# Densely packed edge tiles with per-product tables in a graph transformer layer (gather of 128 message rows per tile, one Trainium2 core)

## What is computed

```python
xn = _layernorm(x, axis=-1)
# graph part: for each edge, HW[col] weighted, added into row
HW = xn @ gnn_W
msgs = edge_weight[:, None] * HW[dst]
AHW = jax.ops.segment_sum(msgs, src, num_segments=N_NODES)
# mix part: q and k through elu+1, k_sum, context = k^T v per head, out = (q context) / (q k_sum), Wproj
x = x + (AHW + gnn_b) + mix(xn, Wq, Wkv, Wproj, bproj)
x = x + ffn(_layernorm(x))      # top 2 of 8 experts, relu
```

## Time and profile before

| | |
|---|---|
| time, median of 3 runs | 3924.36 us (3923.73 to 3926.85) |
| the profiled execution, its own time | 3922.77 us |
| its span (first to last instruction) | 3920.7 us |
| PE busy | 2907.9 us (74%) |
| DVE busy | 2601.0 us (66%) |
| POOL busy | 2537.6 us (65%) |
| ACT busy | 639.4 us (16%) |
| mean granted clock of TensorE | 0.90 of full speed |

### The profile page before, as it was taken

The page is one execution under the profiler, slowest core; times in us unless marked ns, Lnnn a source line. Parts: engine busy times, 40 slices in busy tenths (PEclk is TensorE's granted clock), DMA queues, the critical chain, the costliest instruction groups (busy, mean ns, idle before and its releaser), DMA issues.

```text
span 3920.7 us, 56671 instructions
## 1 busy us (share of the span) xinstructions
PE 2907.9 (74%) x16402; PEld 2390.4 (61%) x16407; DVE 2601.0 (66%) x6332; ACT 639.4 (16%) x1334; POOL 2537.6 (65%) x2431
## 2 busy tenths in 40 slices
PE   5957767376766676766777777777665599999998
PEld 5846666255555555555555555555442488888887
DVE  8899888165555555557888888888767344444444
ACT  8222222310000000000000000000023122222221
POOL 0038888467777777777777777777735777544444
PEclk9997877789898989898998989989877799999999
DMA  5857775634444444434444444444364455544443
GB/s 171 277 166 223 209 212 163 191 105 116 119 119 119 119 118 118 119 114 131 130 130 130 127 128 131 129 131 127 110 209 143 118 119 120 96 72 71 73 71 56
DMA packets 363113, 522.66 MB, mean 133 GB/s; under 512 B 69241, under 2 KB 282749, under 8 KB 363005
## 3 DMA queue, kind: packets, MB, share of 16 engines
q0 software_dynamic: 130944, 275.64, 28.0%
q1 hardware_dynamic: 181523, 190.28, 16.4%
q10 hardware_dynamic: 50537, 55.32, 4.5%
HBM read 378.21 MB, written 140.28 MB: 132 GB/s over the span
## 4 chain that ended last, share of the span: by engine, by line
PE 49%; DVE 12%; issue 10%; POOL 4%; DMA 4%; DVEq 1%; ACT 0%; SPq 0%; POOLq 0%
PE bank L1261 15%; PE bank L1463 10%; PE bank L1476 10%; DVE relu_kq L1951 4%; PE bank L1267 4%; DVE acc L1864 4%; PE bank L1364 4%; DMA message<-h_table,gather_stage 3%; PE bank L1342 2%; POOL x_sorted L781 2%; POOL message L738 2%; PE bank L1362 2%; DVE select L1857 1%; PE bank L1450 1%; DMA read_back<-lists 1%
## 5 line engine op out<-in xcount | busy, mean ns | idle before, releaser
L738 POOL DMA_INDIRECT message<-h_table,gather_stage x1660 | 1598.5, 963 | 558.3 <-issue 488.0
L1261 PE MATMUL bank<-message,select 128*128 128x256 f32 x3320 | 896.8, 418 | 359.4 <-issue 287.8
L1864 DVE TENSOR_TENSOR acc<-acc,bank 128x256 f32 x1660 | 698.9, 421 | 554.3 <-PE bank L1261 390.1
L1261 PEld LDWEIGHTS bank<-message,select 128*128 128x128 f32 x3320 | 661.1, 207 | 553.2 <-issue 368.3
L699 POOL DMA_INDIRECT lists<-placed,dest_i x300 | 381.3, 1271 | 330.1 <-ACT placed L920 244.4
L792 POOL DMA_INDIRECT out<-acc,row_of x224 | 350.1, 1563 | 344.9 <-DVE acc L2157 270.5
L1857 DVE TENSOR_SCALAR select<-iota_n,gather_stage 128x128 f32<-128x128 f32 x1660 | 467.8, 360 | 3.3
L1463 PE MATMUL bank<-fx_t,acc 128*128 128x256 f32 x1792 | 407.6, 381 | 1.6 <-ACT fx_t L1054 1.6
L1476 PE MATMUL bank<-w,acc 128*128 x1792 | 405.2, 379 | 0.0
L1463 PEld LDWEIGHTS bank<-fx_t,acc 128*128 128x128 f32 x1792 | 342.1, 191 | 49.0 <-issue 2.1
L1476 PEld LDWEIGHTS bank<-w,acc 128*128 128x128 f32 x1792 | 331.9, 190 | 40.6
(11 more groups left out here) (304 smaller groups left out, 3648.7 us busy)
## 6 DMA issues: line engine op xcount, KB each, us to landing
rows<-block_dram SPq DMA_DIRECT2D x75, 514.5 KB
acc<-x_sorted SPq DMA_DIRECT2D x112, 260.0 KB, 2.8
message<-h_table,gather_stage POOLq DMA_INDIRECT x1660
xt_in<-xt_dram SPq DMA_DIRECT2D x98, 256.0 KB, 2.9
x_sorted<-blank_rows ACTq DMA_DIRECT2D x42, 390.0 KB
lists<-zeros_list SPq DMA_DIRECT2D x8, 1664.0 KB, 15.4
read_back<-lists SPq DMA_DIRECT2D x13, 1024.0 KB, 6.7
x_sorted<-blank_rows SPq DMA_DIRECT2D x2, 6370.0 KB
```

The costliest lines, as they stand in the source:

```text
L738: pool.indirect_dma_start(out=message[:, slot % SETS, j, :], out_offset=None, in_=h_table, in_offset=Offset(ap=gather_stage[:, slot, j, 0: ...
L1261: last = nc.tensor.matmul(ps, select[:, slot % 2, j, :], message[:, slot % SETS, j, :], start=True, stop=True)
L1864: added = V.tensor_tensor(to, to, ps, ALU.add)
```

## The change

**Packing.** A block now begins at a multiple of 16 edges (`UNIT`) in the sorted list instead of 128. The tiles lie densely: `DENSE` = 1575 tiles hold all edges, and one more, which is empty, serves as filler, so 1576 tiles are gathered, in 394 sets (`GSETS`). A tile may hold edges of two or more blocks. It is then multiplied once per block, each time with another selection matrix. The number of products is fixed at `TT` = 1672, in 418 sets. The row number of an edge in its record now has 10 bits (block modulo 8, and row), and the selection compares it with a 128-column window of a 1024-column ramp (`iota_n`), which starts at the block's key.

**Tables.** Which tile, which block and which message slot a product uses is no longer known when the kernel is written. DVE makes six rows of integers on the chip (`rows_of`), one word per product or set: `acc_row` (offset in `acc`), `key_row` (window of the ramp), `record_row` (where the tile's records lie), `message_row` (its slot in `message`), `need_row` (how far each of the four message semaphores must be), and `free_row` (from which product set on a gathered set's slot is free). They are made behind part 0 of the records (`product_rows`), ahead of the other parts.

**Use.** DVE loads four keys and four record places into registers at the head of each set, ahead of its selects, beside the load of offsets that was there. PE loads four message places and four counts ahead of each set's products. POOL loads eight counts every eight sets; its 394 sets are written out one by one instead of in a loop, and it reads `records` directly. SP's copies into `gather_stage` are gone.

```diff
-    TT = -(-((NG * P + NB * (P - 1)) // P) // SET) * SET
+    UNIT, KEYS = 16, 8
+    DENSE = -(-((E + NB * UNIT) // UNIT) // (P // UNIT))
+    GATHERS = -(-(DENSE + 1) // SET) * SET
+    GSETS = GATHERS // SET
+    TT = -(-(DENSE + NB - 1) // SET) * SET
...
+def load_counts(eng, registers, held, row, first, count, low, op_max):
+    eng.load(registers, row[0:1, first:first + count] if isinstance(first, int) else row[0:1, DynSlice(first, count)])
+    for r, h in zip(registers, held):
+        eng.reg_alu(h, r, low, op_max)
+    return held
...
-            with pool.Fori(1, TSETS // RING) as i:
-                for slot in range(RING):
-                    pool.wait_ge(s_list[slot // SETS], i * 16 + 16)
-                    pool.wait_ge(s_agg, i * RING + (slot - SETS + 1))
-                    gather_set(slot)
+            for k in range(GSETS):
+                if k >= SETS:
+                    if (k - SETS) % 8 == 0:
+                        n = min(8, GSETS - k)
+                        free_from = load_counts(pool, free_registers[0:n], free_held[0:n], free_row, k, n, 1, ALU.max)
+                    pool.wait_ge(s_agg, free_from[(k - SETS) % 8])
+                gather_set(k)
...
             def aggregate(k, slot, first=False):
+                at = load_offsets(pe, message_registers, message_row, k * SET, SET, (SETS * SET - 1) * C)
+                need = load_counts(pe, need_registers, need_held, need_row, k * SETS, SETS, 16 * SET, ALU.max)
+                for j in range(SETS):
+                    pe.wait_ge(s_message[j], need[j])
                 pe.wait_ge(s_select, k + 1)
-                    pe.wait_ge(s_message[slot % SETS], (k - slot % SETS) * 16 + 64)
...
-            def select_tile(slot, j):
-                return V.tensor_scalar(select[:, slot % 2, j, :], iota_n[:, :], gather_stage[:, slot, j, 1:2].bitcast(F32),
-                                       gather_stage[:, slot, j, 2:3].bitcast(F32), ALU.is_equal, ALU.mult)
+            def select_tile(slot, j, key, record):
+                return V.tensor_scalar(select[:, slot % 2, j, :], iota_n[:, ds(key, P)], records_f[:, ds(record + 1, 1)],
+                                       records_f[:, ds(record + 2, 1)], ALU.is_equal, ALU.mult)
...
             def set_turn(k, slot, i, first=False):
-                dve.wait_ge(s_list[slot // SETS], i * 16 + 16)
+                keys = load_offsets(dve, key_registers, key_row, k * SET, SET, (KEYS - 1) * P)
+                places = load_offsets(dve, record_registers, record_row, k * SET, SET, DENSE * 3)
                 for j in range(SET):
-                    made = select_tile(slot, j)
+                    made = select_tile(slot, j, keys[j], places[j])
```

`product_rows` is, cut to its kinds of operation (the four pieces of 512 columns come from PE, which sums the blocks' marks over partitions):

```diff
+            def product_rows():
+                for i in range(-(-TT // 512)):
...
+                    steps.done(V.tensor_scalar(acc_row[:, cols], bank[i][0:1, 0:n], -1.0, float(CR), ALU.add, ALU.mult))
+                    steps.done(V.tensor_scalar(key_row[:, cols], bank[i][32:33, 0:n], -1.0, None, ALU.add))
+                    steps.done(V.tensor_tensor(iota_tile[64:128, cols], iota_tile[64:128, cols], bank[i][64:128, 0:n], ALU.subtract))
...
+                steps.done(V.tensor_scalar(record_row, iota_tile[64:65, :], 3.0, None, ALU.mult))
...
+                for j in range(SETS):
+                    steps.done(V.tensor_scalar(needs[:, :, j], tile_of, float(SET * (SETS - j)), None, ALU.add))
```

More of the change, by code:

```diff
@@ L547, in bring_x @@
                     sp.dma_start(x_in[:, half, :, :], x_pairs[ds(pair, 1), :, :, :].rearrange("a p u c -> p (a u) c")).then_inc(s_x_in[half], 16)
[L549 to L555, removed]
             def stage_context(i, half):
[L558 removed]
+                sp.wait_ge(s_v_psum, i * 2 + (half - 1))
+                bring_xt(i * 2 + (half - 1), half)
             def stage_mix(i, half):
[L561 removed]
+                sp.wait_ge(s_q_psum, i * 2 + (half - MIX_TURN - 2))
+                bring_xt(i * 2 + (half - MIX_TURN - 1), half)
                 bring_x(i, half)
@@ L733, in _, with gather_set @@
             pool.engine_nop().then_inc(s_late, 1)
-            def gather_set(slot):
+            def gather_set(k):
                 pass_gate()
@@ L1260, in aggregate @@
                     ps = bank[(slot % 2) * 2 + j // 2][:, (j % 2) * C:(j % 2 + 1) * C]
-                    last = nc.tensor.matmul(ps, select[:, slot % 2, j, :], message[:, slot % SETS, j, :], start=True, stop=True)
+                    last = nc.tensor.matmul(ps, select[:, slot % 2, j, :], message_flat[:, ds(at[j], C)], start=True, stop=True)
                 last.then_inc(s_agg, 1)
@@ new lines, in _ @@
+            steps.done(V.tensor_scalar(tiles_f[:, 4:5], units_i[:, 1:2], 1.0, None, ALU.min))
+            steps.done(V.tensor_copy(tiles_f[:, 5:6], units_i[:, 2:3]))
+            steps.settle()
+            steps.done(V.tensor_scalar(tiles_f[:, 6:7], tiles_f[:, 5:6], 1.0 / SET, float(SETS - 1), ALU.mult, ALU.add))
+            V.tensor_copy(both_sums[:, P // 2:P], tiles_f[:, 4:5].to_broadcast([P, P // 2])).then_inc(s_shared, 1)
+            steps.settle()
+            steps.done(V.tensor_scalar(past_set[:, :], iota_tile[:, 0:GSETS], tiles_f[:, 6:7], None, ALU.is_gt))
@@ new lines, in _ @@
+            dve.wait_ge(s_shared_psum, 1)
+            steps.done(V.scalar_tensor_tensor(tiles_f[:, 7:8], bank[0][:, 0:1], tiles_f[:, 4:5], tiles_f[:, 5:6], ALU.add, ALU.add))
+            steps.settle()
+            V.tensor_scalar(past_tile[:, :], iota_tile[:, :], tiles_f[:, 7:8], None, ALU.is_ge).then_inc(s_past, 1)
+            dve.wait_ge(s_set_psum, 1)
+            steps.done(V.tensor_scalar(free_row, bank[5][96:97, 0:GSETS], float(SET - 1), None, ALU.add))
+            steps.settle()
+            steps.done(V.tensor_single_scalar(free_row, free_row, 2, ALU.logical_shift_right))
```

149 lines of the change are left out of this document (87 added, 62 removed).

## The result

The changed kernel takes **4352.1 us** (median of 3 runs, 4350.8 to 4356.1) against 3924.4: 1.109 times, interval 1.108 to 1.111. The forecast was 4110, range 3980 to 4300. The direction held; the size was off by 242 us.

A forecast was written before the change was run, and what follows sets the result against it. POOL's gathers were taken to bound context turns, a dependent DVE ring with PE the mix turns. Context -35, mix +206, start +3, middle +4 and tail +8 gave +186 on 3922.8, so 4110 us, range 3980 to 4300.

The forecast's parts named there:

- Mechanism: DVE's sets: new loads behind the last add and later first adds give 4.64 us per set, mix turns +206 us.
- the front part: Head of each DVE set: two loads and a register operation, 1.33 us, beside only the last add; +1.0 us per set.
- the back part: DVE, first select to first add: register addresses stop the sequencer running ahead; 1.65 us instead of 1.04, +0.6 per set.
- I stay with 0.344: DVE's four-word loads: 0.344 us each, from 353 loads between 0.339 and 0.359, against 1.19 in another row.
- Context turns, -35: Context turns: DVE 18.7 us, POOL 18.88, nearly equal; taken as 19.3 instead of 20.03, -35 us in 48 turns.
- The lateness is swallowed: Mix turn, slot 0: adds done by 5.1 us, while the pair's add waits for PE until 5.54 anyway.
- PE at nothing: PE's two loads per set, at most 3.2 us, cost nothing because its sequencer waits for DVE.
- POOL's loads: POOL's counts, once in eight sets: at most 0.2 us per set, hidden in the mix turns.
- Start, middle, tail: Making the six rows +3 us, the turn of the mixing weights +4, the tail's 22 sets +8.
- loads covered: Rival: DVE's sequencer runs ahead, mix turn stays 20.5 us, context turn 18.88; 3868 us, chance 0.09.
- instruction fetch: Rival: DVE's longer loops are fetched anew each pass, two 1.9 us stalls, 179 us more; 4290 us, chance 0.12.
- loads slower than their row: Remaining case: loads take longer than the row they were priced from; chance 0.02.

The follow-up runs named there:

- Loads-once: Changed kernel with keys and record places loaded once ahead of the loop, so address arithmetic vanished too: 3896 us, 0.993 times the kernel before on a clean chip.
- the run with fixed addresses: Changed kernel, all DVE loads kept, but selects read ramp window and record at fixed addresses: 1.053 and 1.045 times the kernel before, both on stalled chips.
- The moved table: Changed kernel with record_row moved from partition 64 to 32, behind the keys: 4184.0 us, 1.066 times the kernel before on a clean chip.
- loads between adds: Changed kernel with DVE's three loads issued one set ahead, each behind one of the first three adds: 4047.3 us, 1.031 times the kernel before.
- the first experiment: Kernel before with two more four-word loads from tile_row at the head of each DVE set, words only kept: 1.034 times, stalled chip.

## Why the prediction was off

- **Mechanism: right.** Loads behind the last add and a held-back load of offsets on DVE lengthen its set and with it the mix turn. Loads-once (0.993 times) and the loads added to the kernel before (1.034) show the front part from both sides, the run with fixed addresses the back part.
- **The step that failed, a term that was mis-sized: "I stay with 0.344".** It was read from loads of an engine that only ever read one table. With tables on both sides of partition 64, two of three loads took 0.56, and a set of DVE 5.28 us instead of 4.64. The moved table measures the term: 168 of the 242 us. The row of `xtile_row` at 1.19 us, which I had as the argument against, is no price for it.
- **The rest, 74 us**, is left when all loads are at 0.34 as I assumed: 4184 against 4110. Its set was 4.83 instead of 4.64. Its selects begin 1.55 us after the last add began, not 1.33, and most of that is the register operations behind the new loads, 0.20 each, not 0.12; its first add 1.62 after the first select, as put (1.65). The mix turn came to 26.0 instead of 24.8 (58 us), the context turn to 19.6 instead of 19.3 (17 us).
- **Context turns, -35.** The sign was wrong: +69. A near tie was the wrong place for confidence. With DVE at 21.4 it was none; the turn rose by 1.4 us. With the near tables it fell, but by 0.4 only, and by 1.0 with loads between adds, where it is close to POOL's 18.9, as worked out.
- **"The lateness is swallowed".** In the profile after, slot 0's adds end at 6.07 us after the product, later than the pair's add (5.54) was due, so only part of the cover was there. The walk from there, with what was put in brackets: selects of slot 1 +2.5 (+1.3), of slot 2 +4.8 (+2.9), of slot 3 +6.3 (+3.65), the next product +7.1 (+4.3), in the turn that begins at 2411.02.
- **PE at nothing: right.** So were POOL's loads (eight words in 0.57 us, once in eight sets). **Start, middle, tail**: +7, +1, +20 where +3, +4, +8 were put; the tail's 22 sets run at DVE's 5.3, not at 4.7.
- **Rivals**: loads covered, out; instruction fetch, out (3 and 11 packets in 24 passes), though its price was by luck the nearest to the result. The Trainium skill, "Runtime: NRT & Kernel Launch", section "Instruction fetch mechanics", has a fetch when a taken branch leaves a window of two pages of 256 instructions. A loop of 273 lies over three pages only if it begins near the end of one, so the trace doesn't speak against the page; the prediction made too much of it. The page's 200 ns for each register, 0.8 us for four, doesn't agree with the rows: 0.33 to 0.56.
- The range ended at 4300 since loads slower than their row had a chance of 0.02, though the only other rows for a load, 1.19 and 1.41 us, were far above. That doubt deserved the width.

## What to carry to other kernels

A register load is cheap only where the sequencer has something to wait for: beside queued datapath work, or between operations that wait for each other. Ahead of the group that everything waits for, its whole length is on the path; move it up one iteration before counting it as free. Keep the tables that one engine reads in turn on the same side of partition 64, and price an operation by rows in the same surroundings, not only of the same kind. When a group of work changes engine, look first at what it then queues behind.

## What was not expected of the hardware

- A load of four words takes 0.34 us, but 0.56 on DVE (0.31 and 0.48 on ACT) when the load before it on the engine read a row on the other side of partition 64. Rows in partitions 0 and 32 read in turn by DVE, and in 64 and 96 by PE, gave loads of 0.33 to 0.35 us; rows in 32 and 64, at the same distance, gave 0.56 on DVE. On the upper side DVE and ACT read partition 64 alone, so a row of theirs in 96 is not tested; why it is so stays open.
- On several chips the sequencers of more than one engine stand still, at times at the same moment, in steps of some 0.7 us, in every kernel run there. POOL's gathers can go on meanwhile: in the first experiment they started 1.25 us apart while DVE stood for 6.0 us. The kernel before took 12 to 13% longer there, and kernels with more sequencer work in their loops did not lose in the same proportion (1.066 on a clean chip was 1.091 and 1.094 there). What causes it stays open.
